# Edge passes of a graph network: one 32-bit scatter product per tile in place of three 16-bit ones, and another sharing of the edge transfers

## The reference

```python
# block 0: five layers, msg per edge from two small MLPs
h = leaky(x @ W1[l] + b1[l]) @ W2[l] + b2[l]            # nodes
e = leaky(edge_attr @ We1[l] + be1[l]) @ We2[l] + be2[l] # edges
agg = segment_sum(h[src] * e * dot_scale[l], dst, n)
# block 1: graph convolution, degrees and segment_sum(h[src], dst)
# block 2: two transformer convolutions (softmax over the edges of a dst)
# block 3: segment_sum(relu(x[src] + edge_attr_64), dst), added to x
```

## Time and profile before

| | us |
|---|---|
| median of three runs | 7169.51 |
| profiled execution | 7184.49 |
| its span (the timeline below) | 7182.9 |
| PE (matmul) busy | 5688.4 (79%) |
| PEld (weight load) busy | 4758.0 (66%) |
| DVE busy | 4863.4 (68%) |
| ACT busy | 2678.6 (37%) |
| POOL busy | 2758.3 (38%) |
| gather products, L1287, 41472 | 2073.8 |
| scatter products, L1296, 20736 | 1866.7 |
| message multiply, L1790, 360 of 1024 float32 elements | 440.6 (1.224 each) |
| subtractions, L1804 and L1810, 432 each | 526.4 and 525.1 (1.219 and 1.215 each) |

### The profile page before, as it was taken

The page is one execution under the profiler, slowest core; times in us unless marked ns, Lnnn a source line. Parts: engine busy times, 40 slices in busy tenths (PEclk is TensorE's granted clock), DMA queues, the critical chain, the costliest instruction groups (busy, mean ns, idle before and its releaser), DMA issues. The chain is left out here.

```text
span 7182.9 us, 255993 instructions
## 1 busy us (share of the span) xinstructions
PE 5688.4 (79%) x87510; PEld 4758.0 (66%) x87511; DVE 4863.4 (68%) x10450; ACT 2678.6 (37%) x5126; POOL 2758.3 (38%) x4136
## 2 busy tenths in 40 slices
PE   4888888846666488788787887887979998999787
PEld 3666666624444288688687786886957776777687
DVE  7555555588888677677677676777755554555688
ACT  2444444424444432222222322323643332333443
POOL 1777777853333155355354453551000000000254
PEclk9999998965656599799798897997779998999999
DMA  2677766622222467476475575664531111111376
GB/s 71 199 197 198 199 198 194 199 69 47 47 47 47 161 168 175 117 176 174 116 175 144 146 175 127 166 173 124 197 121 65 58 63 48 59 62 65 89 192 155
DMA packets 1265072, 933.90 MB, mean 130 GB/s; under 512 B 1003190, under 2 KB 1033581, under 8 KB 1255227
## 3 DMA queue, kind: packets, MB, share of 16 engines
q1 hardware_dynamic: 794406, 635.39, 29.8%
q0 software_dynamic: 224768, 240.90, 13.9%
q10 hardware_dynamic: 245652, 54.13, 3.9%
HBM read 673.72 MB, written 255.19 MB: 129 GB/s over the span
## 5 line engine op out<-in xcount | busy, mean ns | idle before, releaser
L548 POOL DMA_DIRECT2D big<-rows x2592 | 1385.8, 535 | 3287.8 <-issue 2140.5
L1287 PE MATMUL ps<-big 128*128 128x64 bf16 x41472 | 2073.8, 198 | 438.8 <-DMA big<-ohsD 235.2
L1287 PEld LDWEIGHTS ps<-big 128*128 128x128 fp8e4 x41472 | 1793.8, 102 | 482.4 <-issue 478.7
L1296 PE MATMUL ps<-big 128*128 128x64 bf16 x20736 | 1866.7, 203 | 28.0 <-issue 26.9
L1296 PEld LDWEIGHTS ps<-big 128*128 128x128 bf16 x20736 | 1270.5, 118 | 41.1 <-issue 33.7
L1004 ACT COPY big<-big 128x384 bf16 x1728 | 754.9, 508 | 1453.9 <-DVE big L1790 1383.7
L792 POOL DMA_INDIRECT rows<-big x800 | 1066.7, 1333 | 438.7 <-issue 365.2
L1790 DVE TENSOR_TENSOR big<-ps,big 128x1024 f32<-128x1024 f32 x360 | 440.6, 1224 | 514.2 <-PE ps L1287 514.1
L1577 DVE SCALAR_TENSOR_TENSOR big<-big 128x1000 f32<-128x1000 f32 (+1 forms) x300 | 361.9, 1206 | 573.8 <-ACT big L881 554.8
L1254 PE MATMUL ps<-identb,big 128*128 128x128 bf16 x2304 | 435.0, 288 | 347.0 <-DVE big L1697 187.0
L1205 PEld LDWEIGHTS ps<-big 128*125 128x125 f32 (+1 forms) x4800 | 632.1, 197 | 89.8 <-issue 47.7
(11 more groups left out here) (260 smaller groups left out, 7850.1 us busy)
## 6 DMA issues: line engine op xcount, KB each, us to landing
big<-ohsD SPq DMA_DIRECT2D x432, 512.0 KB, 3.8
big<-rows SPq DMA_DIRECT2D x3456, 32.0 KB, 2.7
big<-rows POOLq DMA_DIRECT2D x2592, 32.0 KB, 3.0
big<-maskD SPq DMA_DIRECT2D x50, 1600.0 KB, 6.7
big<-keyT SPq DMA_DIRECT2D x100, 488.3 KB
maskD<-big SPq DMA_DIRECT2D x25, 1600.0 KB, 6.2
ohsD<-big SPq DMA_DIRECT2D x144, 256.0 KB, 2.0
big<-rows ACTq DMA_DIRECT2D x864, 32.0 KB, 2.6
```

What stands on the lines that cost most here:

```text
L548: eng.dma_start(edge[:, u.r * 2 + k, j, :], rows[bass.ds(at, P), col]).then_inc(landed[u.r], 16)
L1287: last = pe.matmul(pG[g % 4][:, j * D:(j + 1) * D], ohsR[:, g, at:at + P].bitcast(F8), slices[:, g, q, (3 * half + c) * D:(3 * half + c + ...
L1296: last = pe.matmul(pacc[:, bass.ds(at, D)], own[:, j % QUAD, :], upper_half(part(u, c)[:, f:f + D]), start=False, stop=False, skip_group_c ...
```

## The change

The scatter takes one product per tile: the float32 message as it is, with a float32 one-hot as weights. The parts of the message, the two subtractions that made them and their signals go. The message has a buffer `msg`, and the sum before the relu in the last pass a buffer `raw`. The one-hots in `hot` become float32. PE waits for `m_ready` of the pair two turns back, for the new signal `hot_ready` of the pair three turns back, and in the last pass for `hi_ready`. The shares of the edge transfers become three for SP, three for POOL and two for ACT.

```diff
-        parts = carve(PR * 3, 2 * GT * D)
-        hot = carve(PR, 2 * GT * P, dt=BF16)
+        msg = carve(PR, 2 * GT * D)
+        raw = carve(PR, 2 * GT * D)
+        hot = carve(PR, 2 * GT * P)
...
-        SP_SHARE, POOL_SHARE, ACT_SHARE = (0, 4), (4, 7), (7, 8)
+        SP_SHARE, POOL_SHARE, ACT_SHARE = (0, 3), (3, 6), (6, 8)
...
-                    act.activation(part(g, 0), part(g, 1), ACT.Relu).then_inc(hi_ready, 1)
+                    act.activation(msg[:, g.r, :], raw[:, g.r, :], ACT.Relu).then_inc(hi_ready, 1)
...
-                for c in range(3):
-                    f = k * GT * D + j * D
-                    last = pe.matmul(pacc[:, bass.ds(at, D)], own[:, j % QUAD, :], upper_half(part(u, c)[:, f:f + D]),
-                                     start=False, stop=False, skip_group_check=True)
-                return last
-
-            def turn_over(u, v, base, nth):
+                f = k * GT * D + j * D
+                return pe.matmul(pacc[:, bass.ds(at, D)], own[:, j % QUAD, :], msg[:, u.r, f:f + D],
+                                 start=False, stop=False, skip_group_check=True)
+
+            def turn_over(u, v, base, nth, rectified):
 
                 to = u.lag(S_LAG)
+                if u.live(2):
+                    pe.wait_ge(m_ready, base + u.lag(2).i + 1)
                 if u.live(S_LAG):
-                    pe.wait_ge(lo_ready, base + to.i + 1)
-                elif u.live(2):
-                    pe.wait_ge(m_ready, base + u.lag(2).i + 1)
+                    pe.wait_ge(hot_ready, base + to.i + 1)
+                    if rectified:
+                        pe.wait_ge(hi_ready, to.i + 1)
...
-                        dve.tensor_tensor(part(u, 0), got, own, ALU.mult).then_inc(m_ready, 1)
+                        dve.tensor_tensor(msg[:, u.r, :], got, own, ALU.mult).then_inc(m_ready, 1)
                     else:
-                        dve.tensor_tensor(part(u, 1), got, own, ALU.add).then_inc(m_ready, 1)
+                        dve.tensor_tensor(raw[:, u.r, :], got, own, ALU.add).then_inc(m_ready, 1)
 
             def remake(u):
                 if u.live():
-                    same(hot[:, u.r, :], dstl[:, bass.ds(u.i * 2 * GT, 2 * GT)], 2 * GT // QUAD)
-
-            def rest(u, base, kind):
-                if u.live():
-                    if kind == "relu":
-                        dve.wait_ge(hi_ready, u.i + 1)
-                    else:
-                        dve.wait_ge(m_ready, base + u.i + 1)
-                    dve.tensor_tensor(part(u, 1), part(u, 0), upper_half(part(u, 0)), ALU.subtract).then_inc(res_ready, 1)
-
-            def lower(u, base):
-                if u.live(1):
-                    g = u.lag(1)
-                    dve.wait_ge(res_ready, base + g.i + 1)
-                    dve.tensor_tensor(part(g, 2), part(g, 1), upper_half(part(g, 1)), ALU.subtract).then_inc(lo_ready, 1)
+                    same(hot[:, u.r, :], dstl[:, bass.ds(u.i * 2 * GT, 2 * GT)], 2 * GT // QUAD).then_inc(hot_ready, 1)
 
             def all_pairs(base, kind, nth):
                 def body(u):
                     message(u, base, kind, nth)
-                    lower(u, base)
                     remake(u)
-                    rest(u, base, kind)
```

More of the change, by code:

```diff
@@ L402, in graph_kernel @@
         hi_ready = sem("hi_ready")
-        res_ready = sem("res_ready")
-        lo_ready = sem("lo_ready")
+        hot_ready = sem("hot_ready")
         craw_loaded = [sem(f"craw_loaded{r}") for r in range(RAW)]
@@ L469, in flat @@
             return t.rearrange("p w f -> p (w f)")
[L471 to L477, removed]
         def row_of(v, w):
@@ L1323, in turn_over, with all_pairs @@
                     put.then_inc(scattered, 1)
-            def all_pairs(base, nth):
+            def all_pairs(base, nth, rectified):
                 v = []
@@ L1330, in body @@
                         v[:] = blocks(PE, u.i)
-                    turn_over(u, v, base, nth)
+                    turn_over(u, v, base, nth, rectified)
                 steps(pe, body)
@@ L1359, in _ @@
                 hold(pe)
-                all_pairs(l * NPAIR, l)
+                all_pairs(l * NPAIR, l, False)
                 pe.drain().then_inc(summed, 1)
@@ L1477, in _ @@
             pe.wait_ge(tab_lo, LAYERS + 1)
-            all_pairs(LAYERS * NPAIR, LAYERS)
+            all_pairs(LAYERS * NPAIR, LAYERS, True)
             pe.drain().then_inc(summed, 1)
```

## The result

The changed kernel takes 10076.92 us (median of four runs, 10011.29 to 10129.11), against 7176.86 for the kernel before, measured again beside it. The ratio is 1.404, 95% interval 1.395 to 1.413: slower by two fifths. 7600 was forecast and 7400 to 7850 was the range, so the sign was right and the size far off. The profiled execution has a span of 10083.9 us, 2901 longer than before.

The account below looks back on a forecast made before the run. SP's issuing was taken to set the pace, with TensorE close behind and becoming the bound after the change. +408 us for the six passes and +29 for their starts, on the 7169.5 median, gave 7600 us; range 7400 to 7850.

Parts of the forecast that it names:

- SP's queue: Edge passes: SP's issuing sets the pace; moving two of eight issues per pair to ACT cuts a trip from 24.07 to 19.7 us.
- TensorE, scatter: Edge passes: one fp32 product replaces three bf16, priced from the attention stage's loads; tile 0.274 to 0.425 us, +408 us together.
- The bound for the step: Scatter's one-hot loads: reading with a step of four elements adds 0.018 us to each of two, tile at most 0.46 us.
- Rival C: Mixed turns of the edge passes: TensorE's clock stays low, +201 us a pass, 8800 us; chance 0.07.
- The stop in the middle of a pair: TensorE in edge passes: the stop of some 0.3 us while its queue reads addresses goes; staying would cost 130 us.
- VectorE: Edge passes: fp32 one-hots taken at 2.34 us, under 4.2 us per pair with the message multiply, hidden under TensorE's 6.8.
- the new waits: TensorE's waits in edge passes for one-hots and messages of earlier pairs: signals come some 6 us early, cost nothing.
- the starts: Start of each edge pass: ACT's extra issues and offsets delay TensorE's first gather by 4.8 us, six times, +29 us.
- B: Edge-pass scatter: fp32 weight loads hide behind the six gathers, tile 0.305 us, sum -225, 6945 us; chance 0.09.
- D: Edge-pass scatter: half of one load hidden, tile 0.353 to 0.365 us, a tie within 0.5% at 7170 us; chance 0.04.
- the likeliest case: Whole kernel: TensorE becomes the bound of the edge passes at 0.425 us a tile, 7600 us; chance 0.80.

Follow-up runs that it names:

- shares_only: The kernel before with only the edge transfers' shares changed (SP 3, POOL 3, ACT 2): 6917.42 us, ratio 0.964.
- dense: The changed kernel with float32 one-hots stored tile by tile, so TensorE reads the weights without a step: 8091 to 8483 us.
- oldshares: The changed kernel with the edge transfers' shares of the kernel before (SP 4, POOL 3, ACT 1): 10081.20 us.
- dense_prehot: dense, with VectorE writing the one-hots of a pass's first four pairs before its first message: 7685.30, 8087.46, 8110.65 and 8494.74 us.

## Why the prediction was wrong

*SP's queue.* Right in that the new shares take the bound away from it: in shares_only and in the changed kernel SP waits for the others. The 20.08 us of shares_only near the 19.7 are luck, since SP waits in them; without its waits a trip would be some 18.4 us (an estimate: 20.08 less the share of 20.9 in 250).

*TensorE, scatter: the first step that failed.* "The row of the same shape gives" the load: it gave it for weights read without a step, and the 0.425 us is exactly what dense shows. For the kernel as changed the term was mis-sized. The bound for the step was taken as a ratio, 118 to 102, from a bf16 load whose four elements span 8 bytes; with float32 the same four elements span 16, and the pair of loads goes from 0.30 to 0.55 us, the tile from 0.425 to 0.67, far above the bound of 0.46. The Trainium skill (SBUF — State Buffer, Door 1: The DMA port swizzle) has a rule that bears on it: consecutive accesses need two or more hits in a 16-byte line for full bandwidth. The runs agree with that (float32 at 8 bytes nearly free, at 16 not); the sentence that follows there, that float32 may be read with a step of four for free, they contradict: 0.67 us against 0.44 at a step of two.

*The clock: the second step that failed.* Rival C had the right end and was given 0.07. The argument against it was that "no long wait is left in which it could fall". No long wait was needed. In the changed kernel the clock fell in all six passes, some 50 to 230 us into the mixture, with no stop longer than 0.06 us. What stands ahead of each fall is small: a turn of the loop, one in some 43 us, at which two tiles are together 0.17 to 0.29 us longer than 0.67 each. Within some 3 us of that the clock is low. In the second pass (the scatter products and some tiles between these lines are left out):

```profile
3687.78 0.34 PE L1279 MATMUL ps<-big 128*128 128x64 bf16 x6
...
3688.45 0.34 PE L1279 MATMUL ps<-big 128*128 128x64 bf16 x6
...
3689.22 0.34 PE L1279 MATMUL ps<-big 128*128 128x64 bf16 x6
...
3689.96 0.34 PE L1279 MATMUL ps<-big 128*128 128x64 bf16 x6
...
3692.03 0.52 PE L1279 MATMUL ps<-big 128*128 128x64 bf16 x6
```

The tiles take 0.67, 0.77 and 0.74 us, and the gather at 3692.03 already runs at the low clock. Four turns earlier in that pass lengthened two tiles as much, and the clock stayed at 1.00. A turn goes ahead of each fall, here and in the six passes of oldshares, but what makes one turn bring it and another not stays open. C's price failed too: it multiplied the whole tile by 1/0.70, and the tile at the low clock came to 0.82.

*How the 2901 us come about.* With dense weights and, by the steps of 400 read under dense_prehot, no pass at the low clock the change takes 7685 us, 516 over the kernel before; forecast were 437. The tile is as forecast; what was not in the sum is a stop of 0.60 to 0.72 us at each turn of the loop, 0.7 x 17 x 6 = 71 us. The stop in the middle of a pair, of which the prediction says that it goes, went, and the one at the loop's turn stayed. In the first pass of dense:

```profile
2611.21 0.34 PE L1279 MATMUL ps<-big 128*128 128x64 bf16 x6 [0.71 <-issue]
...
2639.30 0.34 PE L1279 MATMUL ps<-big 128*128 128x64 bf16 x6 [0.66 <-issue]
```

The other 2392 us, from 7685 to 10077, are the step, by two ways that do not add. If the clock had held, 6624 mixed tiles at 0.67 - 0.425 would cost 1620. As it falls, a tile costs about 0.8 whatever the step. In the profiled execution some 940 tiles ran at the full clock and 5680 at the low one, so the price is 940 x 0.24 + 5680 x 0.39, some 2440 us, less the 71 of stops at the loop's turn, which the changed kernel does not have: 2370 of the 2392. The step's larger harm is that it brings the clock down in every pass.

*VectorE, the new waits, the starts.* Right: 2.28 us against 2.34 taken; TensorE waits for neither one-hots nor messages in mid-pass; the start of a pass costs 4.83 us more, 4.8 forecast. In the time of the changed kernel that term can't be seen, as its runs lie 118 us apart (oldshares).

*Rivals B and D.* Both asked for loads that hide. The timelines show them in the open (the dense tile is the 0.425 without hiding), and their chances were rightly small. Of the 0.80 for the likeliest case too much rested on a row whose operands were laid out otherwise.

## What to carry to other kernels

Price a weight load by the bytes between its elements, not by the shape and type that a row names: widening the type of interleaved operands widens the step too. Before a row at the full clock is used, ask whether the new mixture holds that clock, and put the low one into the range where the answer rests on argument. Two edits in one change can have opposite signs: here the sharing of the transfers alone gains 3.6%, and the scatter beside it hides that.

## What was not expected of the hardware

The edge for a weight load lies between steps of 8 and 16 bytes for both types (bf16: 0.274 us a tile at 8 bytes, 0.37 at 16 and at 32; float32: 0.42 dense, 0.44 at 8, 0.67 at 16). One mixture can hold the full clock and not regain it: the dense float32 tile runs a pass at 1.00 undisturbed, and after a stop of 1.23 us or more mostly stays at 0.50 to the end, and the pass is some 400 us longer. How small a stop stands ahead of a fall depends on the mixture: 1.23 us or more with the dense tile, 0.23 to 0.43 with the seven slow bf16 products, and with the 16-byte float32 step two tiles that are together 0.17 to 0.29 us longer. At the low clock the tile is 0.80 us dense and 0.82 with the step.
